# Attention with heads of 16: a second spare PSUM bank before the first values, stack reads in two transfers per part, third stacks and statistics moved into the first unit

## The reference, cut to what matters

```python
x = x + _L0_xattn_ref(_layernorm(x), ctx_512, ...)   # causal self-attention plus cross-attention, heads of 16
x = x + _L0_ffn_ref(_layernorm(x), ...)
x = x + _L1_xattn_ref(_layernorm(x), ctx_512, ctx_512, ...)   # cross-attention, heads of 16
...
x = x + _L3_xattn_ref(_layernorm(x), ctx_512, ...)            # cross-attention, heads of 16

q = (x @ Wq + bq).reshape(B, LQ, HEADS, D_K).transpose(0, 2, 1, 3)      # D_K = 16
k, v = ...                                                              # the same from the context
out = softmax(q @ k.T / sqrt(D_K)) @ v
return out.transpose(0, 2, 1, 3).reshape(B, LQ, D_MODEL) @ Wo + bo
```

## Time and profile before

| | us |
|---|---|
| median of 3 runs (3411.1 to 3414.0) | 3414.0 |
| profiled execution | 3418.2 |
| its span in the trace | 3416.4 |
| TensorE busy (17261 matmuls) | 2794.7 (82%) |
| VectorE busy | 1979.2 (58%) |
| ScalarE busy | 1440.9 (42%) |
| GpSimd busy | 1142.7 (33%) |

### The profile page before, as it was taken

The page is one execution under the profiler, slowest core; times in us unless marked ns, Lnnn a source line. Parts: engine busy times, 40 slices in busy tenths (PEclk is TensorE's granted clock), DMA queues, the critical chain, the costliest instruction groups (busy, mean ns, idle before and its releaser), DMA issues. The chain is left out here.

```text
span 3416.4 us, 45781 instructions
## 1 busy us (share of the span) xinstructions
PE 2794.7 (82%) x17261; PEld 1597.9 (47%) x17268; DVE 1979.2 (58%) x3631; ACT 1440.9 (42%) x1932; POOL 1142.7 (33%) x1030
## 2 busy tenths in 40 slices
PE   5898887778879789999867899778999998688544
PEld 2343433623336444445743344367777777233222
DVE  3655666577646364445747656664354443577588
ACT  1456556246622244545214455333333432266423
POOL 2233332213232246655315778640010110222333
PEclk7889997879969999999987999799999998699766
DMA  5666561155410001112100000001211221565100
GB/s 143 120 122 128 124 144 34 31 101 125 96 47 1 16 25 44 43 40 75 31 13 1 1 1 1 26 1 29 97 56 48 64 65 50 99 121 103 34 11 15
DMA packets 129740, 198.58 MB, mean 58 GB/s; under 512 B 36272, under 2 KB 66480, under 8 KB 129392
## 3 DMA queue, kind: packets, MB, share of 16 engines
q1 hardware_dynamic: 97776, 143.23, 18.5%
q0 software_dynamic: 31744, 52.41, 5.8%
HBM read 130.73 MB, written 64.75 MB: 57 GB/s over the span
## 5 line engine op out<-in xcount | busy, mean ns | idle before, releaser
L2281 DVE TENSOR_REDUCE L_mx<-bank_t 128x2 f32<-128x1024 f32 (+3 forms) x512 | 565.9, 1122 | 353.1 <-PE bank_t L2092 223.8
L2281 DVE TENSOR_REDUCE L2a_mx<-bank_t 128x2 f32<-128x1024 f32 x256 | 311.2, 1222 | 392.5 <-PE bank_t L2069 391.5
L2488 ACT ACTIVATE L_P<-bank_t 128x1024 f32<-128x1024 f32 (+3 forms) x384 | 340.0, 916 | 248.7 <-PE bank_t L2104 138.1
L2488 ACT ACTIVATE L2a_P<-bank_t 128x1024 f32<-128x1024 f32 x256 | 261.9, 1024 | 285.1 <-PE bank_t L2081 284.8
L2092 PE MATMUL bank_t<-L_KS,L_QS 48*128 48x512 f32 (+2 forms) x1024 | 242.6, 475 | 122.6 <-ACT L_P L2488 50.0
L2069 PE MATMUL bank_t<-L2a_QK 32*128 32x512 f32 x1536 | 252.9, 447 | 71.7 <-ACT L2a_P L2488 28.5
L2104 PE MATMUL bank_t<-L_QS,L_KS 50*128 50x512 f32 (+2 forms) x1024 | 243.2, 478 | 23.4 <-DMA L_QS<-L_spill_max_rows 12.6
L2077 PE MATMUL bank_t<-L2a_QK 32*128 32x512 f32 x1536 | 257.2, 443 | 0.0
L2069 PEld LDWEIGHTS bank_t<-L2a_QK 32*128 32x128 f32 x1536 | 136.9, 197 | 234.3 <-ACT L2a_P L2488 111.6
L2104 PEld LDWEIGHTS bank_t<-L_QS,L_KS 50*128 50x128 f32 x1024 | 100.5, 196 | 258.4 <-issue 170.8
L2134 PE MATMUL bank_o<-L_P,L_V 128*32 128x512 f32 (+3 forms) x1536 | 201.1, 599 | 8.2 <-ACT L_P L2488 7.0
(11 more groups left out here) (444 smaller groups left out, 6184.8 us busy)
## 6 DMA issues: line engine op xcount, KB each, us to landing
L_KS<-L_spill_k_halves SPq DMA_DIRECT2D x174, 128.0 KB, 5.3
L_QS<-L_spill_q_halves SPq DMA_DIRECT2D x174, 128.0 KB, 4.6
L_spill_raw<-xn POOLq DMA_DIRECT2D x64, 256.0 KB, 2.5
L2g_raw<-in_L_ffn_h_blocks SPq DMA_DIRECT2D x32, 512.0 KB, 3.8
L_spill_k_halves<-L_hi SPq DMA_DIRECT2D x32, 256.0 KB, 2.1
L_spill_k_halves<-L_lo SPq DMA_DIRECT2D x32, 256.0 KB, 2.4
L_spill_q_halves<-L_hi SPq DMA_DIRECT2D x32, 256.0 KB, 2.2
L_spill_q_halves<-L_lo SPq DMA_DIRECT2D x32, 256.0 KB, 2.8
```

What stands on the lines that cost most here:

```text
L2281: e.tensor_reduce(neg, s.tile[:, :, 0:n_keys], AX.X, ALU.max, negate=True).then_inc(sem(s.done), 1)
L2488: e.activation(s.at.Pr[s.pb][:, :, q0:S], s.tile[:, :, q0:S], ACT.Exp, scale=s.at.scale).then_inc(sem(s.exp), 1)
```

## The change

It concerns only the stages with heads of 16.

1. `misc` gets a second bank, `bank_o`, until the first value projections are issued; then the bank goes back to the values.
2. The scratch for the halves is laid out by head, high and low parts of a head one after the other. A part of a stack is read by one transfer of 32 partitions and one of 16 instead of three of 16: 4 transfers per stack instead of 6, with the same bytes. The two spills of a stack write to 8 blocks of 16 rows with gaps, where they wrote 128 rows in a run.
3. `begun` becomes a chore that follows unit 1's stacks, among the Smax of unit 0.
4. Ahead of the loop stand 3 Smax of unit 1 and the first value projections. The statistics, now one piece per batch and one for the roots, and the stacks of unit 2 are chores of the first unit, in which each tick may take one.

```diff
             def rest(self):
-                if None in self.e_stats:
-                    self.stats(self.e_stats.index(None), B)
+                if None not in self.e_stats:
+                    return []
+                b0 = self.e_stats.index(None)
+
+                def roots():
+                    self.e_stats[b0:B] = [root(TB * b0, TB * B)] * (B - b0)
+                return [lambda b=b: rows_stats(lambda t: X[:, t, :], self.loaded, TB * b, TB * b + TB)
+                        for b in range(b0, B)] + [roots]
...
-                split_dram = {w: scratch(f"{w}_halves", [2, P, S], 3) for w in "qk"}
+                split_dram = {w: scratch(f"{w}_halves", [P // D, 2, D, S], 3) for w in "qk"}
...
-            o_free, misc = [ALL.free[6]], Banks([bank_m[:, :]])
-            misc.free = [ALL.free[7]]
+            o_free, misc = [ALL.free[6]], Banks([bank_m[:, :], bank_o[:, :]][:2 if D == 16 else 1])
+            misc.free = [ALL.free[7], ALL.free[6]][:2 if D == 16 else 1]
...
-                at_ = landing(n=3 * st.q_of)
+                at_ = landing(n=2 * st.q_of)
...
             if D == 16:
                 add(StackRest(st, st.ready, st.v_ones))
                 chores += prepare(units[1])
+                if begun is not None:
+                    chores.append(lambda: begun(misc))
             else:
                 if norm is not None:
-                    chores.append(norm.rest)
+                    chores += norm.rest()
...
             run_all()
-            add_fed(feed(lead, lead))
             if D == 16:
-                if begun is not None:
-                    begun(misc)
+                add_fed(feed(unit_ticks + 3, 3))
                 chores += value_steps(units[0])
+                run_all()
+                o_free[0] = misc.free.pop()
+                misc.aps.pop()
                 if norm is not None:
-                    chores.append(norm.rest)
+                    chores += norm.rest()
                 chores += prepare(units[2]) + value_steps(units[1])
-                run_all()
+            else:
+                add_fed(feed(lead, lead))
...
-                                run_due(chore=any_tick or p == at.GP - 1 or (pooled and len(chores) > 2))
+                                begins = D == 16 and un.n == 0
+                                run_due(not begins, begins or any_tick or p == at.GP - 1 or (pooled and len(chores) > 2))
...
                 elif kind is SpillStack:
...
-                    e.dma_start(s.spill[0], s.at.hi[s.s][:, :].bitcast(F32)).then_inc(sem(s.landing.done), 16)
-                    e.dma_start(s.spill[1], s.at.lo[s.s][:, :].bitcast(F32)).then_inc(sem(s.landing.done), 16)
+                    e.dma_start(s.spill[:, 0, :, :], s.at.hi[s.s][:, :].bitcast(F32)).then_inc(sem(s.landing.done), 16)
+                    e.dma_start(s.spill[:, 1, :, :], s.at.lo[s.s][:, :].bitcast(F32)).then_inc(sem(s.landing.done), 16)
                 elif kind is ReadStack:
...
-                    for r, part in enumerate((0, 0, 1) if s.which == "q" else (0, 1, 0)):
-                        halves = s.spill[part].rearrange("(s q d) n -> q d s n", q=st.q_of, d=D)
-                        for q in range(st.q_of):
-                            row = st.part * q + D * r
-                            e.dma_start(stack[row:row + D, s.slots, :].bitcast(F32),
-                                        halves[q][:, s.slots, :]).then_inc(sem(s.landing.done), 16)
+                    halves = s.spill.rearrange("(s q) r d n -> q (r d) s n", q=st.q_of)
+                    both, high = (0, 2 * D) if s.which == "q" else (D, 0)
+                    for q in range(st.q_of):
+                        row, mine = st.part * q, halves[q][:, s.slots, :]
+                        e.dma_start(stack[row + both:row + both + 2 * D, s.slots, :].bitcast(F32), mine).then_inc(
+                            sem(s.landing.done), 16)
+                        e.dma_start(stack[row + high:row + high + D, s.slots, :].bitcast(F32), mine[0:D]).then_inc(
+                            sem(s.landing.done), 16)
```

## The result

The changed kernel takes 3456.4 us (median of four runs, 3438.9 to 3463.6) against 3412.6 for the kernel before, measured beside it. The ratio is 1.0124 with an interval of 1.0092 to 1.0157: slower by 1.2%, where 0.7% faster was forecast. The profiled execution has a span of 3461.9 us, 45.5 more than before.

A forecast was written before the change was run, and what follows sets the result against it. TensorE was taken to bound most of the kernel, and a chain from projection to score matmul the openings. Terms -5.2 - 2.3 - 18.6 + 3.5 = -22.6 us gave 3395.6 from the profiled 3418.2, forecast as 3391 for the median, range 3377 to 3408.

The forecast's parts named there:

- slow spill: Second rival: spills in 8 blocks take longer by 3 us or more, delaying stacks; 3424 us, chance 0.07.
- First stacks: Openings of L0, L1, L3: fewer read issues and a second bank against dearer spills; -0.8, -2.2, -2.2, sum -5.2 us.
- Second stacks: Unit 1's first Smax: somewhat faster reads shorten its waits; L0 -2.1, L1 -0.7, L3 +0.5, sum -2.3 us.
- The stretch ahead of the logits: Work and idle time leaving the stretch before the first logits: L0 -9.6, L1 -3.0, L3 -6.0, sum -18.6 us.
- charges for the first unit: Costs set against that stretch's gain for work moved into the first unit: L0 1.0, L1 3.7, L3 5.2 us.
- Third stacks: Projected inside the first unit, may return late for their Smax: L3 +2.5, L0 +1.0, L1 0, sum +3.5 us.
- third rival: First units of L1 and L3 grow by what was taken out, stalls 5 longer; 3405 us, chance 0.12.

The follow-up runs named there:

- spill_only: The kernel before with the scratch by head and spills in 8 blocks, but six reads of 16 partitions as before: 3444.0 us, ratio 1.0098.
- transfers_only: The kernel before with only the change's scratch, spills and reads, the order of the work untouched: 3438.0 us, ratio 1.0076.
- old_transfers: The changed kernel with scratch, spills and reads as before the change: 3419.4 us, ratio 1.0020 to the kernel before.
- before_interleaved: The kernel before with each row's high and low parts side by side in scratch, 128-row spills, fewer or wider reads: 3404.3 us, ratio 0.9980.
- stats_ahead: `interleaved` with only the statistics back ahead of the first logits, unit 2's stacks staying in the first unit: 3410.3 us, ratio 0.9998 to the kernel before.
- moved_only: The kernel before with only the statistics and unit 2's stacks moved into the first unit, a chore each tick: 3444.8 us, ratio 1.0101.
- interleaved: The changed kernel with each row's high and low parts side by side in scratch, 128-row spills: 3413.4 us, ratio 1.0008 to the kernel before.

## Why the prediction was wrong

Forecast 3391, range 3377 to 3408, measured 3456.4. Three steps failed. The sum of -22.6 us covers the openings with their first units; there the table measures -57 + 76 = +19. It has no term for the units behind, where the table measures +26. And within the first part, the charge for the work moved into the first unit was far too small, and the slow spill was taken for an unlikely rival. By steps:

- **First stacks** (-5.2): right in sign, too large. From the k projection to the first Smax, in us:

| | L0 | L1 | L3 |
|---|---|---|---|
| before | 19.4 | 16.7 | 18.0 |
| changed kernel | 19.3 | 16.0 | 17.0 |
| `spill_only` | 21.6 | 18.6 | 20.0 |
| `transfers_only` | 18.9 | 17.9 | 19.7 |
| `old_transfers` | 19.8 | 13.7 | 15.7 |

The changed kernel wins 1.9 us here. The spill was taken at +1.0 us a stage and costs about 2 (`spill_only` against before). The bank brings more than its 1.4 us in L1 and L3 (3.0 and 2.3, `old_transfers` against before), the fewer issues less than 1.8 a stage (2.7, 0.7 and 0.3, `spill_only` against `transfers_only`). The failing step is the choice of the nearer row, "because the same queue and the same 2 KB rows make the first row the nearer one". Queue and row length were not what sets a spill's time; its outermost size was. The waits for the first query stack grew from 12.4, 10.8 and 11.1 to 13.1, 13.2 and 12.6, where they were told to shrink; but they now begin earlier, since the q projection no longer waits, so they are not a measure of the loss.

- **The spills of the later units** (no term): this is the larger part of what the spills cost, 33 of 44 us between the changed kernel and `old_transfers`. The prediction said that "The change can only act in these openings", though every unit's stacks go through the same spills. A wait of 2.0 us, as in the fifth units of L1 and L3, costs 5.9.
- **Second stacks** (-2.3): the reads are faster, as said: 211 and 249 against 129 and 137 GB/s. (The Trainium skill, page "SBUF — State Buffer", section "Door 1: The DMA port swizzle (why `[64,N]` ≈ `[32,N]`)", gives 189 for 32 partitions and 104 for 16; the direction agrees, the measured rates are above its figures.) The waits of 5.46, 2.18 and 0.30 us are 5.34, 2.56 and 3.79 after the change, in L0 with the turns moved ahead of it: +3.8 in all, with the slow spills ahead of the reads. With the interleaved transfers alone (`before_interleaved`) the wait in L0 is 4.80, so the term was taken too large even without slow spills.
- **The stretch ahead of the logits** (-18.6, counted net of the first unit): the opening shrank by 57 us gross, the first logits of L0 came at 68.8 where about 67 was told. The charges for the first unit, 1.0, 3.7 and 5.2 us on top of the moved work, were far too small: the first units grew by 21.7, 19.7 and 34.7. They were drawn from VectorE's work alone, which is the smaller part by `stats_ahead`. Left out were the single bank, in which what follows a projection of the loop waits for ScalarE behind an exponential (4.7 + 2.0 us in L3), and the clock, 0.69 in place of 0.88 over the unit. The charge in L3 did name a clock of 0.50 at the unit's start, but gave it no price of its own. TensorE's busy time is 42.9 us in place of 26.2, moved matmuls included. `moved_only` measures the move by itself, with the new pace of chores: +34 us where the prediction had a gain.
- **Third stacks** (+3.5): the stall was named and its place was right, 5.6 us in L3 (2.5 taken), 0.9 in L1 (0), and in L0 as a wait of 3.9 for `L_hi`, since ScalarE itself waited 3.0 us for an old spill to free its buffer. With the old spills the same wait in L3 is 4.8, with the interleaved ones 2.7, so the late projection makes most of it and not the slow spill.
- **Rivals.** The slow spills, at a chance of 0.07 and a time of 3424, did happen, by the mechanism named and by the rule of the Trainium skill (page "DMA: Bandwidth & Descriptors") of which the prediction said that it "speaks against this change". Its price of 27 is close to the 28 and 32 of `transfers_only` and `spill_only` by luck: it was counted as three spills of 3 us in each opening, where `spill_only` loses about 2 us to the first stack of a stage, and most of the loss is in units that it left out. The third rival, the gain absorbed in the first unit, was priced 14 us above the forecast, and by `moved_only` alone (+34 against before) the move is dearer than what it takes out. Both came together, and no case held that. They were treated as alternatives, though nothing in the profile tied one to the absence of the other.

## What to carry to other kernels

Look at the outermost size on both sides of a transfer before changing a layout: here a write of 256 KB with 8 blocks outermost moved at half of the rate, and what the reader of the layout gained was lost by its writer. Price such a transfer in every unit that issues it, not only where the engines wait for it today. Work moved from an opening that waits into a loop that is bound does not vanish there; here it paid for a bank and its evictions in the loop's order, and a stack projected later landed later. First give the opening what it lacks (here a bank that nobody used yet), and see whether there is anything left to move: this gave 43 us with the interleaved transfers, and the move took them away again.

## What the runs showed of the hardware

- Spills of 8x16x512 (256 KB) kept the DMA share at 0.52 and moved 189 GB/s, those of 128x512 had 1.01 and 383. The issue of one took 0.57 to 0.63 us on SP's queue in the opening of L3, where one of 128x512 takes 0.32 to 0.43.
- Stack reads of 32 and 16 partitions together ran at 211 and 249 GB/s, those of 16 alone at 129 and 137. Reads of 16 rows into every second of 32 partitions (two in three, the third into adjacent ones) landed in 3.9 us, where adjacent ones took 5.3.
- A wait of 2.0 us in a loop that otherwise keeps TensorE busy was followed by a clock of 0.50 for about 8 us. It cost 5.9 us in all, twice, in L1 and in L3. Not every such wait does this: in `interleaved` a wait of 2.03 us in L1 (ending at 721.74 us) stood between windows at 1.00.
